# Last image's softmax and attention by row halves, 0/1 matrices straight from the counts, and VectorE's last round reordered

## What is computed

```
h = edges(x)                                  # 8 x 256 x 256
h = layernorm(h + attention(h))               # Q, K, V with bias, causal softmax
idx = argmax(softmax(t @ Wr)); pos = running count of idx, in token order
kept = pos < 320
out = relu(ein @ W1[e]) @ W2[e]               # ein: the kept tokens of expert e
comb = where(kept, out[slot], t) * where(kept, pmax, 1)
h = layernorm(h + comb)
```

## Time and profile before

| | |
|---|---|
| median of 3 runs | 263.02 us (262.73 to 263.95) |
| profiled execution | 263.28 us, span of its instructions 261.5 us |
| TensorE busy | 244.8 us, 94% of the span |
| VectorE busy | 181.6 us, 69% |
| ScalarE busy | 155.1 us, 59% |
| GpSimd busy | 96.8 us, 37% |
| mean granted clock of TensorE | 0.978 of full |

### The profile page before, as it was taken

How to read it: one execution, slowest core, us unless ns; L and a number is a source line. 1 busy time by engine, 2 the same in 40 slices (tenths; PEclk the granted TensorE clock), 3 DMA queues, 4 the chain that set the end, 5 groups by cost and what they waited for, 6 DMA issues and landing times.

```text
span 261.5 us, 5032 instructions
## 1 busy us (share of the span) xinstructions
PE 244.8 (94%) x1700; PEld 228.4 (87%) x1700; DVE 181.6 (69%) x546; ACT 155.1 (59%) x350; POOL 96.8 (37%) x172
## 2 busy tenths in 40 slices
PE   6999999999999999969999999999999999999930
PEld 5999898988989898647999999999999999999930
DVE  4875496786869696891565796767967778777530
ACT  4335457686867666752745667475774748656400
POOL 6000225656555563636000024034250332513473
PEclk9999999999999999998999999999999999999985
DMA  6847563173993020041898807327082460100000
GB/s 194 276 122 236 146 180 122 44 266 98 287 392 124 5 80 0 29 131 55 221 322 258 277 0 247 126 81 274 0 286 88 137 217 1 45 3 20 10 27 0
DMA packets 28122, 35.48 MB, mean 136 GB/s; under 512 B 2652, under 2 KB 24907, under 8 KB 28098
## 3 DMA queue, kind: packets, MB, share of 16 engines
q1 hardware_dynamic: 26016, 31.71, 38.1%
q0 software_dynamic: 1792, 3.47, 3.7%
q10 hardware_dynamic: 290, 0.00, 0.1%
HBM read 26.97 MB, written 9.47 MB: 139 GB/s over the span
## 4 chain that ended last, share of the span: by engine, by line
PE 49%; POOL 2%; issue 2%; DMA 1%; ACT 1%; DVE 1%; POOLq 1%; SPq 0%; DVEq 0%
PE bank L1163 14%; PE bank L1165 14%; PE bank L1164 14%; PE bank L1393 3%; PE bank L1444 2%; POOL out_dram L549 1%; PE bank L1367 1%; DMA images<-dispatched 1%; PE bank L1325 1%; PE bank L1377 1%; POOL yrstd L572 1%; POOLq L67 1%; ACT trow L662 0%; ACT lone L671 0%; POOL ynmr L573 0%
## 5 line engine op out<-in xcount | busy, mean ns | idle before, releaser
L1092 DVE SCALAR_TENSOR_TENSOR h_lo<-bank,h_hi 128x320 fp32r<-128x320 f32 x58 | 28.4, 489 | 29.9 <-ACT h_hi L759 27.1
L759 ACT ACTIVATE h_hi<-bank 128x320 fp32r<-128x320 f32 x58 | 25.3, 437 | 40.1 <-PE bank L1165 40.1
L1163 PE MATMUL bank<-einT_hi,w_hi 128*128 128x320 f32 x128 | 40.4, 316 | 0.2 <-DVE h_lo L1092 0.2
L1165 PE MATMUL bank<-einT_hi,w_lo 128*128 128x320 f32 x128 | 39.6, 309 | 0.0
L1164 PE MATMUL bank<-einT_lo,w_hi 128*128 128x320 f32 x128 | 39.5, 309 | 0.0
L896 DVE TENSOR_TENSOR w_lo<-w_raw,w_hi 128x1024 fp32r<-128x1024 f32 x32 | 38.8, 1214 | 0.0
L549 POOL DMA_INDIRECT out_dram<-tokens_mem,images x24 | 27.4, 1143 | 28.4 <-ACT tokens_mem L776 22.2
L1163 PE MATMUL bank<-h_hi,w_hi 128*128 128x320 f32 x112 | 35.3, 316 | 0.0
L1164 PE MATMUL bank<-h_lo,w_hi 128*128 128x320 f32 x112 | 34.6, 309 | 0.0
L1165 PE MATMUL bank<-h_hi,w_lo 128*128 128x320 f32 x112 | 34.6, 309 | 0.0
L694 ACT ACTIVATE w_hi<-w_raw 128x1024 fp32r<-128x1024 f32 x32 | 33.7, 1054 | 0.0
(11 more groups left out here) (210 smaller groups left out, 590.3 us busy)
## 6 DMA issues: line engine op xcount, KB each, us to landing
w_raw<-in_L_ffn_W_dram SPq DMA_DIRECT2D x16, 1024.0 KB, 7.9
images<-in_x_dram SPq DMA_DIRECT2D x7, 768.0 KB, 4.8
dispatched<-blank SPq DMA_DIRECT2D x4, 645.0 KB, 8.3
images<-dispatched SPq DMA_DIRECT2D x9, 258.0 KB, 3.9
out_dram<-lone SPq DMA_DIRECT2D x8, 256.0 KB, 3.9
images<-in_x_dram SPq DMA_DIRECT2D x2, 384.0 KB, 5.9
images<-dispatched SPq DMA_DIRECT2D x9, 64.5 KB, 3.8
out_dram<-tokens_mem,images POOLq DMA_INDIRECT x24, 3.6
```

What stands on the lines that cost most here:

```text
L759: act.activation(hidden_halves(n)[0], bank[n % 2][:, 0:CAP], ACT.Relu).then_inc(h_hi_ready, 1)
L1092: dve.scalar_tensor_tensor(lo, bank[n % 2][:, 0:CAP], 0.0, hi.bitcast(F32), ALU.max, ALU.subtract).then_inc(h_ready, 1)
L1163: pe.matmul(to, ah, bh, start=first, stop=False)
L1165: return pe.matmul(to, al, bh, start=False, stop=last)
```

## The change

- SyncE issues the load of expert 0's rows before `store_lone(5)`.
- The index row starts at 1, so that the 0/1 matrices of images 6 and 7 are made straight from the counts of expert 0 (`mine[:, s, 0:1]`), before the slots are worked out; `placed` goes.
- For the last image softmax, transposes and attention go by row halves, the long half (`s` = 1, 256 keys) first, with semaphores of their own.
- VectorE's line of the last round is written out in another order, and so is ScalarE's.
- `split_high(0)` and `split_low(0)` move from round 6 to 5, piece 1 from round 7 and the tail to round 6; piece 2 goes to the end of ScalarE's tail and, on VectorE, among the experts.
- TensorE: 4 dummies instead of 7 before the last transposes, none instead of 2 before the last attention, none instead of 3 before `place(7)`, 2 instead of 4 behind it; `count(7)` moves behind `early_turn`.

```diff
@@ SyncE
+                if i == L:
+                    for b in range(L - 1 - TR, L - 1):
+                        sp.wait_ge(rows_out[b % TR], 16 * SC * (b // TR + 1))
+                    load_rows(0)
                 if 2 <= i < B + 1:
                     store_lone(i - 2)
-                if i == L:
-                    for b in range(L - 1 - TR, L - 1):
-                        sp.wait_ge(rows_out[b % TR], 16 * SC * (b // TR + 1))
-                    load_rows(0)
@@ GpSimd
-            step(pool.iota(slot_index, pattern=[[1, CAP]], base=0, channel_multiplier=0,
+            step(pool.iota(slot_index, pattern=[[1, CAP]], base=1, channel_multiplier=0,
@@ ScalarE
+            def late_probs():
+                act.wait_ge(pT_done, L)
+                for n, s in enumerate((1, 0)):
+                    act.wait_ge(nbias_ready, SC * L + n + 1)
+                    act.activation(prob[:, s, 0:(s + 1) * P], score[:, s, 0:(s + 1) * P], ACT.Exp,
+                                   bias=nbias[:, s:s + 1], scale=-1.0, accum_out=psumr[:, L % 2, s:s + 1]
+                                   ).then_inc(late_probs_ready, 1)
+
+            def late_prob_t():
+                act.wait_ge(pT_done, L + 1)
+                act.wait_ge(attn_done, L)
+                act.activation(probT[:, P:3 * P], bank[7][:, P:3 * P], ACT.Copy).then_inc(probT_ready, 1)
+                act.wait_ge(late_turned, 1)
+                act.activation(probT[:, 0:P], bank[3][:, 0:P], ACT.Copy).then_inc(late_probT_ready, 1)
...
+            late_probs()
+            late_prob_t()
+            norm_rows(L - 1)
+            route_exp(L - 1)
             norm_lone(L - 2)
             norm_lone(L - 1)
-            split_high(2)
             norm_rows(L)
             route_exp(L)
+            split_high(2)
@@ VectorE, softmax_max
+                if b == L:
+                    dve.wait_ge(rowc_ready, b + 1)
+                    for n, s in enumerate((1, 0)):
+                        m = (s + 1) * P
+                        dve.tensor_tensor_reduce(score[:, s, 0:m], bank[6][:, s * S:s * S + m],
+                                                 causal[:, S - m:S], -SCALE, -MASKED, ALU.add, ALU.min,
+                                                 nmax[:, s:s + 1]).then_inc(nmax_ready, 1)
+                        dve.wait_ge(nmax_ready, SC * b + n + 1)
+                        dve.tensor_scalar(nbias[:, s:s + 1], nmax[:, s:s + 1], rowc[:, s:s + 1], rowc[:, s:s + 1],
+                                          ALU.subtract, ALU.add).then_inc(nbias_ready, 1)
+                    return
@@ VectorE, assign
+                if b >= L - 1:
+                    for s in range(SC):
+                        dve.tensor_scalar(pick(b, s), slot_index, mine[:, s, 0:1], None, ALU.is_equal
+                                          ).then_inc(pick_ready, 1)
                 link(dve.tensor_reduce(place[:, :], mine[:, :, :], AX_X, ALU.add))
...
-                if b >= L - 1:
-                    link(dve.tensor_tensor(placed[:, :], basep[:, :], over[:, :], ALU.add))
-                    for s in range(SC):
-                        dve.tensor_scalar(pick(b, s), slot_index, placed[:, s:s + 1], None, ALU.is_equal
-                                          ).then_inc(pick_ready, 1)
@@ VectorE, order of the last round
+            route(L - 1)
+            factor(L - 2)
+            residual(L - 1)
+            residual_in(L, 0)
+            residual_in(L, 1)
+            keys_low(L)
+            moments(L - 1)
+            softmax_max(L)
+            assign(L - 1)
+            softmax_sum(L)
             residual(L)
+            moments(L)
             factor(L - 1)
             route(L)
-            moments(L)
             assign(L)
-            split_low(1)
             factor(L)
-            split_low(2)
...
-                    if j in (0, 1) and 4 * e + j > 0:
+                    if j in (0, 1):
                         split_low(4 * e + 2 + j)
@@ TensorE
-            keep_warm(7)
-            prob_t(L)
-            keep_warm(2)
-            attend(L)
+            keep_warm(4)
+
+            def late_prob_t():
+                pe.wait_ge(late_probs_ready, 1)
+                pe.wait_ge(resid_ready, SC * L)
+                pe.wait_ge(onehot_ready, L)
+                pe.transpose(bank[7][:, P:2 * P], prob[:, 1, 0:P], ident[:, :])
+                pe.transpose(bank[7][:, 2 * P:3 * P], prob[:, 1, P:2 * P], ident[:, :]).then_inc(pT_done, 1)
+                pe.wait_ge(late_probs_ready, 2)
+                pe.transpose(bank[3][:, 0:P], prob[:, 0, 0:P], ident[:, :]).then_inc(late_turned, 1)
+
+            def late_attend():
+                pe.wait_ge(probT_ready, L + 1)
+                pe.matmul(bank[5][:, 0:XG], probT[:, P:2 * P], val[:, L % 2, 0, 0:XG], start=True, stop=False)
+                pe.matmul(bank[5][:, 0:XG], probT[:, 2 * P:3 * P], val[:, L % 2, 1, 0:XG], start=False, stop=True
+                          ).then_inc(late_attn_done, 1)
+                pe.wait_ge(late_probT_ready, 1)
+                pe.matmul(bank[7][:, 0:XG], probT[:, 0:P], val[:, L % 2, 0, 0:XG], start=True, stop=True
+                          ).then_inc(attn_done, 1)
...
             place(L - 1)
+            early_turn()
             count(L)
-            early_turn()
-            keep_warm(3)
             place(L)
-            keep_warm(4)
+            keep_warm(2)
```

More of the change, by code:

```diff
@@ L208, in vit_tower_kernel @@
         slot_index = tokens_mem[:, 8 * D:8 * D + CAP]
-        placed = sb("placed", [P, SC])
         def pick(b, s):
@@ L228, in vit_tower_kernel @@
         mean_done = sem("mean_done")
+        late_probs_ready = sem("late_probs_ready")
+        late_turned = sem("late_turned")
+        late_probT_ready = sem("late_probT_ready")
+        late_attn_done = sem("late_attn_done")
         pick_ready = sem("pick_ready")
@@ L382, in _ @@
                     load_first((i - 2) // 2) if i % 2 == 0 else load_second((i - 2) // 2)
-                if 2 <= i < B + 1:
-                    store_lone(i - 2)
                 if i == L:
@@ L388, in _ @@
                     load_rows(0)
+                if 2 <= i < B + 1:
+                    store_lone(i - 2)
             for i in range(TR):
@@ L724, in _ @@
                     scale_blue(i + 2)
-                else:
-                    split_high(i + 2 - B)
-                if 2 <= i < L:
+                elif i < L:
+                    split_high(1)
+                if i == L:
+                    break
+                if i >= 2:
                     norm_lone(i - 2)
                 probs(i)
-                if i < L:
-                    edges(i + 1, 0)
+                edges(i + 1, 0)
+                if i == L - 2:
+                    split_high(0)
                 prob_t(i)
-                if i < L:
-                    edges(i + 1, 1)
+                edges(i + 1, 1)
                 if i >= 1:
                     route_exp(i - 1)
-                if i < L:
-                    tokens_high(i + 1)
+                tokens_high(i + 1)
                 if i >= 1:
                     norm_rows(i - 1)
+            late_probs()
+            late_prob_t()
+            norm_rows(L - 1)
+            route_exp(L - 1)
             norm_lone(L - 2)
             norm_lone(L - 1)
-            split_high(2)
             norm_rows(L)
             route_exp(L)
+            split_high(2)
             def ein_t(e):
@@ L935, in softmax_sum @@
             def softmax_sum(b):
-                dve.wait_ge(probs_ready, b + 1)
+                if b == L:
+                    dve.wait_ge(late_probs_ready, SC)
+                else:
+                    dve.wait_ge(probs_ready, b + 1)
                 step(dve.reciprocal(rinv[:, b % 2, :], psumr[:, b % 2, :]))
             def residual(b):
-                dve.wait_ge(attn_done, b + 1)
+                dve.wait_ge(late_attn_done if b == L else attn_done, 1 if b == L else b + 1)
                 settle()
@@ L944, in residual @@
                     dve.wait_ge(t_ready, SC * (b - 1))
-                for s, at in enumerate((7, 5)):
+                for s, at in ((1, 5), (0, 7)) if b == L else ((0, 7), (1, 5)):
+                    if b == L and s == 0:
+                        dve.wait_ge(attn_done, b + 1)
                     dve.scalar_tensor_tensor(resid[:, b % 2, s, :], bank[at][:, 0:D],
@@ L950, in moments @@
             def moments(b):
-                for s in range(SC):
-                    dve.wait_ge(resid_ready, SC * b + s + 1)
+                for n, s in enumerate((1, 0) if b == L else (0, 1)):
+                    dve.wait_ge(resid_ready, SC * b + n + 1)
                     step(dve.bn_stats(stats[:, s, :], resid[:, b % 2, s, :]))
@@ L1046, in _ @@
             dve.wait_ge(pool_const, 3)
-            for i in range(B):
+            for i in range(L):
                 if i >= 1:
@@ L1066, in _ @@
                     red_and_green(i + 2)
-                elif i < L:
-                    split_low(0)
```

(21 more changed lines are left out.)

## The result

The changed kernel took a median of 262.12 us (259.72 to 262.66, 9 executions), the kernel before 263.40 us beside it (262.73 to 266.7, 9). The ratio is 0.9937, with a 95% interval of 0.9909 to 0.9965: some 1.6 us faster (the two medians lie 1.3 us apart). The forecast was 3.6 us and 259.5 us, with a range up to 262.0, so the time lies just outside it. Ratios here leave out executions over 1.5% above the fastest of the same kernel, among them those of the kernel before at 266.5 to 267.0 us, four of e3 and one each of e4, e7 and e8; medians and the times in brackets are of all.

A forecast was written before the change was run, and what follows sets the result against it. TensorE is nearly always busy from the experts' first Relu on, so the start of that stretch counts. -3.9 us there and +0.3 for split_low(2) make -3.6: 259.5 us predicted, range 258.6 to 262.0.

The forecast's parts named there:

- Step 1: SyncE's load of expert 0's rows is issued at 107.8 us instead of 111.79 and lands at about 111.0.
- Step 2: The earlier weight splits fit idle time of ScalarE and VectorE in round 5: taken as zero, bounds 0 and 1.2 us.
- Steps 3 and 4: Last image: VectorE's new order delays the row maximum 0.9 us, softmax and attention by halves give it back, leaving +0.1.
- step 4: Softmax and attention by halves for the last image: +0.1 us left after the reorder's cost, bounds -0.3 and +0.9.
- Steps 5 and 6: early_turn without its wait ends 2.55 us earlier; count(7) behind it and fewer dummies start place(7) at 115.8, 3.05 earlier.
- Step 7: place(7) at full clock ends at 118.15 us; the experts' first Relu comes at 119.7 instead of 123.57, -3.9.
- Rival A: The tail's half-clock stretch moves instead of vanishing and loses 1.7 us: gain 1.9, time 261.2 us; chance 0.17.
- Step 8: split_low(2) on VectorE among the experts delays the first expert_out: cost 0.3 us, bounds 0 and 1.2.
- Rival B: The last image's halves gain nothing, so the reorder's 0.9 us passes through: 260.3 us; chance 0.10.
- Rival C: The experts start earlier, then wait for expert 2's weights (margin 0.6 us): 262.2 us; chance 0.07.
- Rival D: Slower: half clock stays on from place(6) through the first experts; 10 us of it give 264.5 us; chance 0.04.
- The three signs: Wrong if half clock lies in 108 to 125, round 5 exceeds 12 us, or a Relu waits behind a transfer-bound split.

The follow-up runs named there:

- e3: Changed kernel with piece 0's splits back in round 6 and piece 1's in round 7 and the tail: 260.0 us, ratio 0.9878 to the kernel before.
- e4: Kernel before with only the load of expert 0's rows moved ahead of the store of image 5's lone rows: 260.71 us, ratio 0.9913.
- e7: Changed kernel with the last image's softmax, transposes and attention whole as before, VectorE's new order kept: 262.63 us, ratio 0.9953 to the kernel before.
- e8: Changed kernel with piece 0's low split behind round 5's token sum and piece 2's ahead of the experts: 259.78 us, ratio 0.9857 to the kernel before.
- e6: Changed kernel with the load of expert 0's rows put back behind the store of image 5's lone rows: 266.65 us, ratio 1.0105 to the kernel before.
- e17: Changed kernel, unedited, one more profiled execution: 261.77 us, half clock in the tail.
- e18: Changed kernel, unedited, one more profiled execution: 261.68 us, half clock in the tail.
- e5: Changed kernel, unedited, timed again: 261.85 us, ratio 0.9953 to the kernel before; its profiled execution took 259.78 us.
- e11: Changed kernel with e8's split placement, e9's mixed start and three dummies between count(7) and place(7): 259.95 us, ratio 0.9875 to the kernel before.
- e9: Changed kernel with the start's 256-column products laid between its one-column products: 261.97 us, ratio 0.9935 to the kernel before.
- e10: Kernel before with the start's 256-column products laid between its one-column products: 263.93 us, ratio 1.0038 to the unedited kernel before.
- e2: Kernel before with four 512-column dummies among the start's one-column products: 265.32 us, ratio 1.0097 to the unedited kernel before.
- e12: Kernel before, unedited, one more trace: 262.53 us, half clock in the tail and full clock at the start.
- e16: One of four more profiled executions of the kernel of e6, which took 266.73, 265.44, 265.78 and 265.80 us.
- e1: Changed kernel with four 512-column dummies among the start's one-column products: 261.44 us, ratio 0.9958 to the kernel before.

## Why the prediction was partly right and partly wrong

**Step 1 (the load moved) holds,** and carries nearly the whole gain of the tail: alone it gives 3.80 us there (e4), and without it nothing is left (e6).

**Step 2 (the earlier splits at zero) failed: +0.8 us.** I looked for idle time on VectorE's and ScalarE's own lines, found 1.21 us, and called the split covered. It was covered on its own engine. What I did not look at is that GpSimd adds the blue plane in exactly this idle time. With the split beside it the addition takes 2.11 us instead of 1.28, and the token sum behind it 1.61 instead of 0.77, which is all of the 0.8 us by which round 5 grew; apart from it both keep their length (e3, e8). The upper bound of 1.2 us was in the range, the value was at the wrong end. The Trainium skill ("SBUF — State Buffer", section "SBUF: two separate sides") says that VectorE and GpSimd share a pair of ports under an exclusive lock: a VectorE instruction with two inputs in that memory and a GpSimd instruction that reads it exclude each other, and the loser waits for the other's whole length. The trace agrees in the order of events and nearly in size: the addition starts at 88.55 beside the split, and ends 1.12 us behind the split's end at 89.54 (alone it takes 1.27); the token sum ends at 91.21, 0.55 behind the addition (alone 0.77). By that rule step 2 would have been no zero.

**Steps 3 and 4 (the reorder and the halves) hold.** Less the 2.83 us by which the tail of the trace after is late, the row maximum starts at 106.26 (109.09; predicted 106.3) and place(6) at 110.11 (112.94; predicted 110.2). The halves alone give 0.5 us (e7) and not the 0.8 of step 4.

**Steps 5 and 6 hold.** There is no wait ahead of early_turn, and place(7) starts at 115.37 by the same reckoning (118.20; predicted 115.8), 0.4 us sooner. One reading in the sum was too short: from the end of the second low part to the first Relu it took 0.48 us, where the trace before has 0.85 (122.72 to 123.57) and the trace after 0.80. The two errors cancel, and the Relu came 0.1 us sooner than predicted.

**Step 7 (place(7) at full clock) failed in most executions: +1.7 us.** Full clock was argued from the gaps, all under 1 us. In e17 and e18 the clock fell 0.2 to 0.3 us after the gap ahead of place(7), of 0.92 us, and place(7) took 4.11 us instead of 2.42. Rival A had the mechanism and its price, 1.7 us, and was given 0.17; in 2 of 4 traces, and by their clock in 12 of 20 executions, it is what happens. In a further quarter the stretch lies at the start, where nothing was forecast, and costs 1.55 us: from the first one-column product to the token sum are 9.87 us in the trace after (9.53 to 19.40) and 8.32 in e17 (8.65 to 16.97) as in the trace before (9.05 to 17.37). (The other 1.17 of the 2.72 us between the trace after and e5 were lost ahead of that product: 9.53 against 8.36.) Only where there is none, 3 of 20, is the time the forecast's. The Trainium skill ("TensorE: Matmul & The Clock Gate", Part 1) says, as cited with rival A, that idle time brings the half state back. In direction e17 and e18 bear that out; it does not tell which execution falls, since after and e5 have the same gap and their clock did not fall there.

**Step 8 (0.3 us) holds:** 0.33, and all of it goes when the split is taken out of there (e8, e11).

**The sum** with the two terms as measured: -3.6, +0.8 and +1.7 make -1.1, so 263.28 becomes 262.2; the median was 262.12. That the two meet so closely is in part luck: the median falls among executions with the tail stretch, and the start of each execution moves the time by some tenths. Had only step 2 been costed rightly, the forecast would have been 260.3.

**Rival B** is false, the halves do gain. **Rival C's** wait exists: ScalarE waits for expert 2's weights in the trace after, as the margin of 0.6 us had warned, and the next Relu stands behind the split, 2.59 us after the last one instead of 1.76 before (142.63 to 145.22; 143.46 to 145.22). But TensorE does not idle for it, and the Relu to the end costs nothing beyond step 8:

```profile
144.25 1.06 ACT L712 ACTIVATE w_hi<-w_raw 128x1024 fp32r<-128x1024 f32 x1 [1.19 <-DMA w_raw<-in_L_ffn_W_dram]
```

**Rival D** did not come; while TensorE works, the longest low stretch of the changed kernel is 3.4 us. With the load left behind the store (e6) it was 10 us long. The three signs by which the prediction wanted to be called wrong were all seen: half clock between 108 and 125 (e17, e18), round 5 over 12 us (12.58), and a Relu behind a split that waits for a transfer (145.22). The third was harmless.

**What decides where the stretch lies** is in part not in the program. Already the first dummies and products of TensorE, which wait for nothing, differ in length between executions, as if they went over from half speed to full speed at different moments. TensorE's timeline after, and under it that of e17 (the same kernel):

```profile
2.61 4.64 PE L1370 MATMUL bank<-w_hi 128*128 128x512 f32 x10
7.05 2.65 PE L1216 MATMUL bank<-wk,wq 128*128 128x256 f32 x8
```

```profile
2.61 4.47 PE L1370 MATMUL bank<-w_hi 128*128 128x512 f32 x10
6.92 1.89 PE L1216 MATMUL bank<-wk,wq 128*128 128x256 f32 x8
```

In the 15 traces with the start unedited, from the first dummy to the first one-column product are 5.75 to 7.01 us. The early stretch came in the three with the most (after 6.92, e4 7.01, e6 6.83), whatever the kernel, and in none of the 12 others (the next has 6.58). In the changed kernel 5.75 us went with no stretch (e5) and 6.04 and 6.05 with the stretch in the tail (e17, e18).

The tail has a sign of the same kind. Between the fall in the tail and the last fall of a trace, behind TensorE's last product, lie 136.53 or 136.54 us in six traces (before, e8, e9, e10, e17, e18), though the first of the two falls comes 3.0 to 5.0 us ahead of the end of place(7). In six others (e2, e12 to e16) it is 139.95. So the falls keep a time of their own, and the program's work lies against it differently in each execution. Counted back by the same 136.54 us from the last fall, this moment is at 117.79 in the trace after, 115.35 in e5, 117.04 in e1 and 115.85 in e7, in each of them inside the gap ahead of place(7) (117.28 to 118.20, 114.59 to 115.51, 116.28 to 117.20, 115.44 to 116.21), and in e3 at 113.37, 0.97 ahead of it; none of these lost clock in the tail. In e8, e9, e17 and e18 the gap was over 0.19 to 0.85 us before the fall. So the same gap brings half clock or not by where it lies against these moments. That is a reading of nine traces and no experiment: no run moved the gap against them and nothing else.

**What stays open** is whether the removed dummies let the clock fall. The kernel before had the stretch in the tail in both its traces, though it has all 16. With all 16 dummies kept (e4) 9 of 12 executions have a clock of 0.987 to 0.989, with them cut 3 of 20; but e7, with the same dummies cut, has 5 of 12, e3 6 of 12 (0.984 or 0.985, as its trace without the stretch), and e1, with dummies only at the start, 8 of 12. For the dummies speaks e11: counted in the same way the moment lies at 114.90, 0.13 us behind the start of place(7), much as in e17, but the gap was filled and the clock stayed. That is one trace. The dummies were not put back alone. Open too are the slowest executions of the kernel before: 19 of 82 took 266.5 to 267.0 us at a mean clock of 0.966 or 0.967, and none of the changed kernel's 20 did. None of them was traced, and the ratios leave them out.

## What to carry to other kernels

Before an instruction is costed at nothing because its engine is idle there, look at what other engines do in that same microsecond, for VectorE at what GpSimd does. When the time of a kernel lies in groups, take several profiles of it and split each span at a few fixed events: one profile here blamed the start, of three more two showed the tail and one nothing. And of a change with many parts time the simplest alone: moving one load gave 3.8 of the tail's 4.0 us, and a kernel no slower than the whole change.

## What the runs showed of the hardware that was not expected

- The half-clock stretch of some 3.4 us is not bound to a place: at 12.0 to 15.4 us in one execution, at 116.0 to 119.5 in another, nowhere in a third (apart from the stretch behind TensorE's last product that all have). At the start it followed 2.3 us of one-column products during which TensorE counts as busy, and the same products left the clock at 1.00 in the other executions.
- The first ten dummies take 4.64 us; in the tail four take 1.17. By their length most of the ten run at about half speed, though the column of the granted clock shows 1.00 there.
- With four dummies at the start the stretch in the tail 100 us later was twice as long (e2: 6.8 us instead of 3.4).
- A GpSimd product of two columns takes 1.06 us instead of 0.20 beside a VectorE subtraction of 1.21 us.
- Four executions of e9, e10 and e11 took 265.5 to 266.1 us at a mean clock of 0.988 or 0.989. In e9 and e11 that is some 6 us above others with the same clock, so something other than the clock costs them; no trace shows it.
